# The last two states of eleven scan runs: input products by TensorE from diagonals of B, and six instead of eight C products of 32 on VectorE

## What is computed

```python
dA = jnp.exp(dt[..., None] * A)
dBx = (dt * x)[..., None] * Bm[:, :, None, :]

def step(h, inputs):
    dA_t, dBx_t, C_t = inputs
    h = dA_t * h + dBx_t
    y = jnp.einsum('bdn,bn->bd', h, C_t)
    return (h, y)
...
return jnp.swapaxes(ys, 0, 1) + x * D[None, None, :]
```

## Time and profile before

| what | us |
|---|---|
| three runs, median (lowest to highest) | 1397.96 (1394.28 to 1404.04) |
| profiled execution, span from first to last instruction | 1398.2 |
| the scan loop inside it, first to last unit on VectorE | about 40 to 921 |
| the expert layer behind it | from about 960 on |

### The profile page before, as it was taken

The page is one execution under the profiler, slowest core; times in us unless marked ns, Lnnn a source line. Parts: engine busy times, 40 slices in busy tenths (PEclk is TensorE's granted clock), DMA queues, the critical chain, the costliest instruction groups (busy, mean ns, idle before and its releaser), DMA issues. The chain is left out here.

```text
span 1398.2 us, 16596 instructions
## 1 busy us (share of the span) xinstructions
PE 1302.0 (93%) x5288; PEld 781.7 (56%) x5288; DVE 938.9 (67%) x1140; ACT 723.7 (52%) x1296; POOL 964.5 (69%) x511
## 2 busy tenths in 40 slices
PE   8999989999998989899798878899999999999997
PEld 3443333344333334333343333457999999999996
DVE  3899999999999999999999999972111111111110
ACT  4888776678785677676767563413111111111111
POOL 1899999999999999999999999831222222222211
PEclk9999999999999999999999999988999999999999
DMA  5555455555555464555456554607988889888882
GB/s 205 182 166 166 162 173 168 166 165 159 182 175 181 145 187 150 166 167 176 159 180 190 184 176 138 192 4 263 381 320 302 322 318 324 306 316 320 316 312 47
DMA packets 105497, 290.40 MB, mean 208 GB/s; under 512 B 9649, under 2 KB 19506, under 8 KB 89922
## 3 DMA queue, kind: packets, MB, share of 16 engines
q1 hardware_dynamic: 95762, 271.24, 55.7%
q0 software_dynamic: 9648, 18.09, 6.4%
HBM read 271.47 MB, written 9.96 MB: 201 GB/s over the span
## 5 line engine op out<-in xcount | busy, mean ns | idle before, releaser
L451 PE MATMUL ps_y<-arena,ident 128*128 128x512 f32 x1020 | 499.7, 622 | 54.6 <-POOL arena L1200 54.4
L1200 POOL TENSOR_TENSOR arena<-arena 128x1024 f32<-128x1024 f32 x192 | 457.4, 2404 | 19.6 <-DVE arena L946 15.5
L451 PEld LDWEIGHTS ps_y<-arena,ident 128*128 128x128 f32 x1020 | 192.1, 196 | 323.2 <-issue 218.4
L1184 POOL TENSOR_TENSOR arena<-arena 128x1024 f32<-128x1024 f32 x127 | 303.8, 2392 | 7.5 <-issue 4.7
L737 ACT ACTIVATE ps_de<-arena,An 128x512 f32<-128x512 f32 x256 | 176.3, 689 | 226.9 <-DVE arena L943 226.2
L1249 POOL DMA_INDIRECT out_x<-arena x39 | 61.8, 1584 | 305.2 <-ACT arena L881 305.2
L927 DVE TENSOR_TENSOR ps_u<-ps_du,arena 128x512 f32<-128x512 f32 x256 | 178.7, 698 | 23.9 <-DVE arena L957 8.6
L1151 DVE TENSOR_TENSOR arena<-ps_du,arena 128x512 f32<-128x512 f32 x39 | 27.0, 692 | 229.7 <-PE ps_du L617 229.7
L737 ACT ACTIVATE arena<-arena,An 128x512 f32<-128x512 f32 x256 | 181.1, 707 | 0.0
L943 DVE TENSOR_TENSOR_SCAN arena<-ps_de,hlast,arena 128x512 f32<-128x512 f32 x128 | 163.1, 1274 | 1.0 <-ACT arena L737 1.0
L943 DVE TENSOR_TENSOR_SCAN arena<-ps_de,arena 128x512 f32<-128x512 f32 x128 | 155.2, 1213 | 3.7 <-ACT arena L737 3.7
(11 more groups left out here) (223 smaller groups left out, 1490.7 us busy)
## 6 DMA issues: line engine op xcount, KB each, us to landing
arena<-bc_scratch SPq DMA_DIRECT2D x256, 512.0 KB, 4.7
arena<-in_W SPq DMA_DIRECT2D x117, 1024.0 KB, 8.1
arena<-arena POOLq DMA_DIRECT2D x15, 512.0 KB, 4.9
arena<-in_xT SPq DMA_DIRECT2D x2, 1024.0 KB, 5.5
arena<-in_w2c SPq DMA_DIRECT2D x1, 2048.0 KB, 8.9
arena<-in_xT SPq DMA_DIRECT2D x4, 512.0 KB, 6.2
X_scratch<-stg SPq DMA_DIRECT2D x12, 128.0 KB, 4.8
out_x<-stg SPq DMA_DIRECT2D x12, 128.0 KB, 5.0
```

Source lines behind the costliest of these rows:

```text
L451: t = e.matmul(Y[j][:, :], ident[:, :], hc[:, i % NP, j, :], start=False, stop=(n == 15))
L1184: e.tensor_tensor(uA[:, turn % 2, :, :], duA.rearrange("p (o t) -> p o t", o=1).to_broadcast([128, 2, TH]), ring[:, turn % NR, 0, :, :], A ...
L1200: e.tensor_tensor(hc[:, i % NP, :, :], hh[:, i % NH, :, :], c, ALU.mult).then_inc(gp_hc, 1)
```

## The change

In runs 2 to 12 (`MADE_RUNS`) the last turn (`MADE_TURN` = 7, units n = 14 and 15) is **made** by TensorE:

- du of both groups is turned: four TensorE transposes each (`turn_du`) into a side bank, and a ScalarE copy to `duT` in SBUF (`turned_du`), at iterations of the table `TURN_AT`, in most runs n = 2 and 3.
- `make_u(i)`: four matmuls of 128 columns for group 1 into `ps_de0` or `ps_de1`, then four for group 0 into `ps_u`. The stationary operand is `duT`, the moving one a 128 x 128 diagonal of B. `make_u(i + 1)` stands in iteration i between `side_work(i)` and `add(i - 2)`.
- The diagonals lie in a DRAM scratch: SyncE clears it with eight DMAs (`clear_diagonals`), writes the values of B onto the diagonals with 24 DMAs of 2 x 128 single elements (`spread`), and `ring_load` reads a full 128 x 2 x 512 block from it for such a turn.
- VectorE drops `u(i)` and GpSimd `u(turn)` for these turns. ScalarE writes the group 1 decay to `uA` there, and the scan takes decay and input in exchanged places.
- du of group 0 of runs 2 to 12 goes to `du0` in SBUF (the space of `wmT`), straight from dt and x in SBUF, two units ahead (before the scans of unit n = 14 of the run before); ScalarE copies it to `ps_du`.
- `OWN_MADE` has VectorE do the C product in units 4, 9, 15, 20, 25, 31 of 32 in these runs (3 in a run, not 4).

```diff
+OWN_MADE = (4, 9, 15, 20, 25, 31)
+MADE_RUNS, MADE_TURN = range(2, 13), 7
+TURN_AT = {16 * r_ + {7: 5, 11: 9, 12: 6}.get(r_, 2) + (1 - j_): (r_, j_) for r_ in MADE_RUNS for j_ in range(2)}
...
+            def turn_du(r, j, banks):
+                if j:
+                    e.wait_ge(gp_du, r + 1)
+                else:
+                    e.wait_ge(dv_du, r + 1)
+                p = take(("duT", r, j), banks)
+                for c in range(4):
+                    x = (duA if j else du0)[:, c * 128:c * 128 + 128]
+                    t = e.transpose(PS[p][:, c * 128:c * 128 + 128], x, ident[:, :])
+                t.then_inc(full[p], 1)
+
+            def make_u(i):
+                turn = i // 2
+                e.wait_ge(l_ring[turn % NR], 32 * (turn // NR + 1))
+                for j in range(2):
+                    is_free(("duT", i // 16, j))
+                e.wait_ge(dv_sA, i - 1)
+                for j in (1, 0):
+                    if j == 0:
+                        e.wait_ge(dv_sB, i)
+                        if own(i - 1):
+                            e.wait_ge(dv_hc, owned(i - 1))
+                    for c in range(4):
+                        t = e.matmul((DE[i % 2] if j else U)[:, c * 128:c * 128 + 128], duT[:, j, c, :],
+                                     ring[:, turn % NR, 0, i % 2, c * 128:c * 128 + 128], start=True, stop=True)
+                    t.then_inc(pe_u1 if j else pe_u0, 1)
...
             for i in range(NU + LAG):
                 if i < NU:
                     side_work(i)
+                if i + 1 < NU and made(i + 1):
+                    make_u(i + 1)
                 if i == NU:
                     out_block(1, 0, 1, both_side, (0, 1))
                 if i >= LAG:
                     add(i - LAG)
+                if i in TURN_AT:
+                    turn_du(*TURN_AT[i], both_side)
...
+                if r == MADE_RUNS[0]:
+                    for m in range(2):
+                        is_full(e, ("x1", 0, m, 1))
+                elif r in MADE_RUNS:
+                    is_full(e, ("duT", r - 1, 0))
+                elif i:
+                    e.wait_ge(ac_dc, r)
                     w = DU[:, :]
-                e.tensor_tensor(DU[:, :], w, xc[q % 2][:, 2 * pr, HB[th]], ALU.mult).then_inc(dv_du, 1)
+                e.tensor_tensor(du0 if r in MADE_RUNS else DU[:, :], w, xc[q % 2][:, 2 * pr, HB[th]], ALU.mult).then_inc(dv_du, 1)
...
             for i in range(NU):
-                if i % 16 == 0:
+                if i % 16 == 0 and i // 16 not in MADE_RUNS:
                     du(i)
-                u(i)
+                if (i + 2) % 16 == 0 and (i + 2) // 16 in MADE_RUNS:
+                    du(i + 2)
+                if not made(i):
+                    u(i)
...
                 for w in range(2):
+                    if w == 0 and made(2 * turn):
+                        e.wait_ge(l_dg[th], 64 * (q + th))
+                        x = dg_dram[q % 2, th, :, 0:128 * TH].rearrange("n (p f) -> p n f", f=TH)
+                        e.dma_start(ring[:, turn % NR, 0, :, :], x).then_inc(l_ring[turn % NR], 16)
+                        continue
...
+            def spread(q, th):
+                e.wait_ge(l_zero, 16 * 8)
+                e.wait_ge(l_bc, 16 * (q + 1) + 16)
+                for c in range(4):
+                    x = bc_dram[q, 2 * MADE_TURN:2 * MADE_TURN + 2, th * TH + c * 128:th * TH + c * 128 + 128]
+                    to = dg_dram[q % 2, th, :, c * 128:c * 128 + 128 * (TH + 1)].rearrange("n (p f) -> n p f", f=TH + 1)
+                    e.dma_start(to[:, :, 0], x, allow_slow_non_contiguous=True).then_inc(l_dg[th], 16)
```

87 lines of the change are left out of this document (70 added, 17 removed).

## The result

The changed kernel takes 1451.76 us (median of 4 runs, 1448.11 to 1460.62), the kernel before 1396.12 on the same chip (4 runs, 1392.42 to 1404.04): ratio 1.041, interval 1.0382 to 1.0437. The forecast was 1405 with a range up to 1423. The profiled execution has a span of 1450.8 us, 52.6 more than before.

What follows compares the result with a forecast made beforehand. The loop was taken to run at VectorE's pace, GpSimd close behind. 1398.2 + 4.9 on VectorE's path + 2 for TensorE's load + 0.1 for SyncE = 1405.2, said as 1405 us; range 1388 to 1423.

Steps and rivals of the forecast that it cites:

- the waits for adds: `OWN` units waiting for TensorE's later add three back, runs 3 to 7: +2 us, bounds 0 and +14.
- +0.1 for SyncE: Eight clears and 24 single-element writes ahead of ring loads: +0.1 us, mostly hidden by the ring's slack, upper end +8.
- The pair: Units 14 and 15: unit 15's wait for TensorE takes what the two dropped `u`, 1.22 us a run, gave.
- Scans at 3.8 and 4.95: Unit 15's scans, in us after unit 13's end, with only an add between; next `u` at 7.15, 0.35 sooner.
- +8.85: Next run's first `u` after unit 13's end, with half a convolution also between: 1.36 us later than before.
- `OWN` unit: VectorE does one C product less in every made run: 0.92 us saved each.
- 20 to 28 us in all: Expected new wait of VectorE's group 1 scan for TensorE `ps_de`, about 11 times, near 0.8 or 2.5 us each.
- about 1 us of lateness: Turned du makes TensorE later in run 4, included in its +2.1 us; one us likewise in run 6, at +0.85.
- about 1 for eight transposes: TensorE's time for turning du in each made run: about 1 us, within 4.6 us of added load.
- The lock: Moved du and GpSimd excluding each other at SBUF: taken at 0, bounds 0 and +22 us; slow rival 1416, chance 0.08.
- TensorE fills up: Rival: added 4.6 us a run exceeds TensorE's idle time, runs 2 to 7 each +3: 1423, half 1414; chance 0.22.
- over 10 was to mean TensorE's load: Sign: line 1050 waiting over 10 us for adds would show TensorE's load, with time over 1412 us.

Runs made afterwards that it cites:

- e1: Kernel before, with only the added wait of `u` for ScalarE's copy of du in runs 2 to 12: 1408.43 us, ratio 1.0092.
- e2: Changed kernel, du turned in run 2 alone, later runs' products using that stale du: 1436.08 us.
- e16: Changed kernel, du turned in run 2 alone and the wait in `u` only at a run's first unit: 1428.69 us, ratio 1.0247.
- e14: Changed kernel, no input product made by TensorE; turning, moved du, wait, `OWN_MADE` and small DMAs stay: 1461.96 us.
- e15: Changed kernel, no input product made by TensorE and du turned in run 2 alone: 1443.87 us.
- e3: Changed kernel, same work, turning moved to slots where the table of takes leaves a side bank free: 1441.19 us.
- e6: Changed kernel, TensorE makes unit 15's group 1 right behind unit 14's products, its group 0 after the add, before side work: 1454.25 us.
- e18: e16 with TensorE's order of e6 besides: 1425.56 us, ratio 1.0211.
- e4: Kernel before, with only the C products of runs 2 to 12 placed as in `OWN_MADE`: 1400.0 us, ratio 1.0028.
- run 5: Not a follow-up kernel: one stretch of 16 units in the scan loop, here of the changed kernel; its pair ends 7.97 us after unit 13.
- e7: Changed kernel, ScalarE copies next dt to `ps_du` at n = 13 in runs 3 to 12, so moved du reads one PSUM input: 1453.74 us.
- e10: Kernel before, group 1's add done twice in five units of each of runs 2 to 12: 1400.42 us, ratio 1.0025.
- e11: Changed kernel, group 1's add left out in five units of each of runs 2 to 12: 1446.65 us.
- e8: Changed kernel with turning moved, wait once a run, unit 15's group 1 ahead of the add, and dt from PSUM together: 1446.84 us, ratio 1.0351.
- e17: e16 with VectorE's C products in all places of the kernel before (`OWN_MADE = OWN`): 1436.06 us, ratio 1.0293.

## Why the prediction was wrong

The direction was forecast, the size missed by 47 us, and the measured time is far outside the range up to 1423. The step that failed is the price of the first 14 units of the made runs. The sum books -8.0 us for them (-10.1 for the C products, +2 for the waits for adds, +0.1 for SyncE); they measured +30.5. That is 38.5 us. The pairs and gaps of runs 2 to 12 are 7 more than forecast (22.0 for 15.0), run 1's pair and gap 4.6 (the forecast had nothing there). Together these are 50 us in the loop, and the 4.4 behind it come off. By its steps:

- **The pair was right in its mechanism, and 7 us too small.** "Scans at 3.8 and 4.95" and "+8.85" for six runs meant 1.36 us more per pair; with the gap, runs 2, 3, 5, 7, 8 and 9 measured 1.5, 3.6, 1.6, 1.5, 3.1 and 1.8 more. Over runs 2 to 12 it is 22 us where my steps (without the `OWN` unit) give 15. VectorE's wait "20 to 28 us in all" is 25.7, and where two matmuls of 512 columns stand between, one such wait is 2.7 to 2.9, save in run 8.
- **The wait in `u` is missing from the sum.** The prediction prices two removed `u` and leaves the other 14 of each run as they were. Those directly behind a scan, 105 in the row above, begin 0.11 us later: e1 +12.9 us, e2 to e16 -7.4 by the medians and -13.5 by the traces. The largest omission that is shown alone.
- **The turning was mis-sized**: "about 1 us of lateness" and "about 1 for eight transposes", with its two side banks not thought of; in the sum it stands with the lateness of runs 4 and 6, some 2 us. It costs 15.7 us (e2) to 18.1 (e14 and e15), most of it by place (e3 -10.6), as in run 8, where ScalarE empties its bank late and TensorE stands for the other.
- **The waits for adds** were put "at +2"; the row went from 4.9 to 21.1. Some of that is the turning's: in e2 the same row is 10.6. e6 and e18 show that this wait and the pair's are partly one: what is taken from the one comes to the other.
- **The `OWN` unit**: 10.1 us were booked for 11 runs. Beside the products the new places bring 9.0 in the first 14 units but 5.5 in the sum; by themselves they cost 4.4 (e4; 2.4 in the loop). That 0.92 of VectorE is saved per product left out doesn't mean that the time is.
- **The lock** was put at 0, "since the wait for TensorE covers it", for ten du. There are eleven: that of run 2 is done in run 1, whose pair is not made and covers nothing. It took 5.24 us and lengthened that pair from 6.0 to 11.0. In run 8 du took 4.49 us, and there the cover held for the most part: VectorE then had no wait for unit 15, and the pair is some 1 us longer than in the like runs (9.1 against 8.1). In the nine others du took its free 0.67 us; in run 5 it starts at 382.04 and GpSimd's product at 382.20, so VectorE won that tie. The Trainium skill, SBUF — State Buffer, section "SBUF: two separate sides", says that the one of the two engines which starts first has their shared ports for the whole of its instruction and the other is blocked until then, VectorE's instructions with two SBUF inputs among them. e7 agrees: with one of its inputs in PSUM the same du took 0.67 us beside GpSimd. But e14 shows a higher price than one instruction: in six of eleven du VectorE lost to GpSimd instructions that started after du had.
- **The rival "TensorE fills up"** named the place that gave way, and its sign came true: line 1050 waits 21.1 us for the adds, where over 10 was to mean TensorE's load. But load alone doesn't stand as the cause: e10 adds 34.8 us of TensorE to the kernel before for some 3 us, and taking 4.3 a run from the changed kernel (e11) gives back 5.1. In e8 it gives back 13.4, so with the other parts gone load does count.

The traces' sum closes by steps, each from the table: changed to e2 13.6, e2 to e16 13.5, e16 to e17 -5.5, e17 to before 35.4; together 57.0. Of the last, 26.1 are the pairs (about 4.6 of it the lock in run 1), 1.0 the gaps, and 8.4 the first 14 units. These 8.4 I did not take apart: the spread DMAs, SyncE's longer queue (`u` waits 3.1 us for ring loads in e17, not at all in the kernel before) and TensorE's lateness behind a pair are all in it.

What stays open is what a part costs beside the others: the wait in `u` gave 2.5, 7.4 or 12.9 us, the C products' places cost 4.4 alone and bring 7.4 in e16, and 4.3 us less of TensorE a run brings 5.1 to the changed kernel, 13.4 to e8 and about 1 to the kernel before. Some of these differ by no more than the noise. e6 and e18 show one reason: time taken out ahead of unit 15 can come back behind it. That the engines are coupled within a unit or two in the made runs, so that one wait can hide another, would fit the rest, but was not tested by itself. No version of the change made here beats the kernel before.

## What to carry to other kernels

An engine that may run three units behind costs next to nothing while only sums come from it (34.8 us more of it cost some 3 us in e10); give it one product that the critical engine needs at once, and all its backlog stands on the path at that point. Before moving work to it, ask what is in its queue there, and which shared banks the new steps take: a bank that is missed once in a queue stopped four engines for 7 to 10 us. And count every wait that a change adds to an instruction repeated hundreds of times, fulfilled or not: look whether it stands directly behind the instruction whose end it follows.

## What the runs showed of the hardware

**A fulfilled wait isn't free where it stands between two instructions that follow each other at once.** In e1 the added wait, on a semaphore whose count had been reached before, moved the 116 `u` directly behind a scan by 0.11 us each (1.29 to 1.40), 13 us in all for the 12.9 measured. The 60 `u` behind other instructions didn't move.

**An instruction that loses the lock can lose it three times in a row, or only once.** From e14, VectorE and then GpSimd:

```profile
375.89 5.83 DVE L1000 TENSOR_TENSOR wmT<-arena 128x512 f32<-128x512 f32 x1
```

```profile
375.12 4.82 POOL L1300 TENSOR_TENSOR arena<-arena 128x1024 f32<-128x1024 f32 x2
379.75 1.41 POOL L1269 TENSOR_TENSOR arena<-arena 128x512 f32<-128x512 f32 x1
381.24 2.70 POOL L1284 TENSOR_TENSOR arena<-arena 128x1024 f32<-128x1024 f32 x1
```

du starts at 375.89, while GpSimd has its first of two products, and does not get in between the first and the second, nor between the second and du of group 1 at 379.75; that ends at 381.16, and VectorE's ends 0.56 behind it, at 381.72. Two runs later in the same kernel, VectorE and then GpSimd:

```profile
504.54 1.18 DVE L1000 TENSOR_TENSOR wmT<-arena 128x512 f32<-128x512 f32 x1
```

```profile
502.80 5.12 POOL L1300 TENSOR_TENSOR arena<-arena 128x1024 f32<-128x1024 f32 x2
```

Here du gets in between the two products, which take 5.12 us together and not 4.8. Five of e14's du did so and six did not; what decides it no run here shows. So the price of a lost tie lies between the rest of one instruction of the other engine and all that stand there without a wait: 4.93 to 6.79 us in the six.

**Writes of single elements occupy the issuing queue for longer than large loads.** The 24 writes of 256 elements of 4 bytes, ahead of ring loads, and the ring loads of 512 KB themselves (ns min/median/max):

```profile
L1424 SPq DMA_DIRECT2D dg_scratch<-bc_scratch x24: 596/1258/3668, 132.5 to 705.3; - x24
L1410 SPq DMA_DIRECT2D arena<-bc_scratch x245: 359/466/1543, 30.6 to 959.8; - x123
```

At the median a write of 1 KB in single elements takes 1.26 us of SyncE's queue and a load of 512 KB 0.47. What this costs the kernel was not tested by itself.
